# A Mamba-2 layer with a mixture of experts: where rows are finished, the last store goes out, and routing work stands

## What is computed

```python
xn = layernorm(x)                              # input of both branches
zxbcdt = xn @ in_proj_w.T                      # z 1024, x 1024, B 128, C 128, dt 16 (heads of 64)
xBC = silu(conv_b + causal_conv(xBC, 4 taps)); dt = softplus(dt + dt_bias)
# scan by chunks: Y_diag = ((C Bt) * L) (x dt);  Y_off = C state * exp(cumsum);  state = state * decay + Bt (x dt)
y = rmsnorm((Y_diag + Y_off + x * D) * silu(z)) * norm_w
attn = y @ out_proj_w.T
experts = sum over the top 2 of 8 experts of  weight * down(silu(gate(xn)) * up(xn))
out = x + attn + experts
```

## Time and profile before

| | us |
|---|---|
| runs, median of 3 | 699.69 (699.25 to 702.23) |
| profiled execution, its own time | 697.2 |
| its span | 695.2 |
| TensorE busy | 637.0 (92%) |
| VectorE busy | 507.8 (73%) |
| ScalarE busy | 373.6 (54%) |
| GpSimd busy | 294.0 (42%) |
| chain that ended last: TensorE, VectorE, issue, DMA | 61%, 17%, 7%, 7% |

### The profile page before, as it was taken

The page is one execution under the profiler, slowest core; times in us unless marked ns, Lnnn a source line. Parts: engine busy times, 40 slices in busy tenths (PEclk is TensorE's granted clock), DMA queues, the critical chain, the costliest instruction groups (busy, mean ns, idle before and its releaser), DMA issues.

```text
span 695.2 us, 12667 instructions
## 1 busy us (share of the span) xinstructions
PE 637.0 (92%) x4215; PEld 522.4 (75%) x4216; DVE 507.8 (73%) x1098; ACT 373.6 (54%) x787; POOL 294.0 (42%) x209
## 2 busy tenths in 40 slices
PE   4998899999999999989999989898988899999991
PEld 3896687868879678776877967665677788899981
DVE  6998868877977887787797698999786644444430
ACT  4778936564654754557376373638245444444431
POOL 2011344526435454453544424341136665656641
PEclk9999999999999999999999999998999999999996
DMA  8672014305113131530412304083594766767663
GB/s 269 231 288 92 1 39 145 122 11 173 60 64 122 62 123 32 151 123 1 152 51 103 96 28 130 1 272 115 172 305 80 132 123 117 125 120 123 125 100 45
DMA packets 31890, 80.38 MB, mean 116 GB/s; under 512 B 4768, under 2 KB 10016, under 8 KB 29664
## 3 DMA queue, kind: packets, MB, share of 16 engines
q1 hardware_dynamic: 22784, 58.23, 25.4%
q0 software_dynamic: 9056, 21.50, 17.1%
HBM read 59.93 MB, written 19.79 MB: 115 GB/s over the span
## 4 chain that ended last, share of the span: by engine, by line
PE 61%; DVE 17%; issue 7%; DMA 7%; ACT 5%; POOL 2%; SPq 0%; DVEq 0%; ACTq 0%; POOLq 0%
PE pi L1471 17%; PE po L1510 11%; PE pg L1685 9%; PE pd L1698 7%; DVE xs L959 5%; PE py L1566 3%; PE py L1573 3%; PE px L1668 2%; DMA out<-yo,idx 2%; DVE y L1244 2%; PE pxb L1557 2%; PE pxb L1588 2%; ACT m L675 1%; DMA m<-cs_d 1%; DMA out<-o 1%
## 5 line engine op out<-in xcount | busy, mean ns | idle before, releaser
L1471 PE MATMUL pi<-xh,whl 128*128 128x256 f32 x1152 | 165.1, 286 | 1.8 <-DVE zs L965 1.3
L1471 PEld LDWEIGHTS pi<-xh,whl 128*128 128x128 f32 x1152 | 146.3, 188 | 4.6 <-issue 2.4
L959 DVE SCALAR_TENSOR_TENSOR xs<-raw,conv_w,xs 128x256 f32<-128x256 f32 x240 | 112.1, 532 | 11.0 <-ACT xs L650 10.9
L1510 PE MATMUL po<-wo,y 128*128 128x512 f32 x256 | 114.8, 602 | 0.5 <-DVE y L1256 0.5
L1471 PE MATMUL pi<-xl,whl 128*128 128x256 f32 x576 | 91.7, 281 | 0.0
L1510 PEld LDWEIGHTS po<-wo,y 128*128 128x128 f32 x256 | 48.1, 193 | 55.4 <-issue 55.2
L551 POOL DMA_INDIRECT out<-yo,idx x39 | 62.0, 1590 | 61.2 <-ACT yo L817 32.4
L675 ACT ACTIVATE m<-m,cs_tok 128x128 f32<-128x128 f32 x256 | 79.7, 389 | 0.5
L1471 PEld LDWEIGHTS pi<-xl,whl 128*128 128x128 f32 x576 | 78.4, 188 | 0.0
L1685 PE MATMUL pg<-ew,xgh 128*128 x312 | 64.6, 349 | 0.0
L524 POOL TENSOR_TENSOR carry<-carry,cd 128x1024 f32<-128x1024 f32 x14 | 27.8, 1987 | 79.6 <-PE py L1566 79.6
(11 more groups left out here) (220 smaller groups left out, 1161.9 us busy)
## 6 DMA issues: line engine op xcount, KB each, us to landing
m<-cs_d SPq DMA_DIRECT2D x16, 1024.0 KB, 6.5
e<-cs_d SPq DMA_DIRECT2D x30, 256.0 KB, 4.6
ew<-in_w_gu SPq DMA_DIRECT2D x8, 768.0 KB, 9.5
w_as_read<-in_w_in SPq DMA_DIRECT2D x9, 512.0 KB, 8.3
res<-in_x SPq DMA_DIRECT2D x16, 256.0 KB, 2.8
out<-o SPq DMA_DIRECT2D x16, 256.0 KB, 2.0
xin<-in_x SPq DMA_DIRECT2D x6, 512.0 KB, 3.6
xn_d<-xin SPq DMA_DIRECT2D x6, 512.0 KB, 2.8
```

The lines of the kernel that those rows point to most:

```text
L959: dve.scalar_tensor_tensor(out=xs[par][:, b, :], in0=raw[:, b, k:k + GT], scalar=conv_w[:, b, k:k + 1], in1=xs[par][:, b, :], op0=ALU.mult ...
L1471: mm = pe.matmul(bank[:, hf, :], whl[:, weight(g, n), lo, k, hf * P:(hf + 1) * P], xx[:, k, :], start=k3 == 0, stop=k3 == 11)
L1510: mm = pe.matmul(po[:, :], y[:, b, :], wo[:, b, :], start=b == 0, stop=b == XB - 1)
```

## The change

- `finish(t - 1)` of the even tiles 2 to 12 stands behind `carried()` instead of ahead of `own(1)`. SyncE's `store(t - 1)` and `load_res(t)` of these tiles move into the next tile, behind its decay loads.
- ScalarE casts the weights of expert 0 in tile 15 behind the copy of B, not at the end of tile 14.
- `probabilities()` stands at the end of tile 13. `experts_of_tiles()` goes to tile 15, in two parts, around the last-but-one `finish`.
- Gathers 2 and 3 write to two buffers of their own, over the second x buffer, and wait for the scan's last read of it (yd = 32). Gathers 4 and 5 go ahead of the loop and wait for the transposes of tiles 0 and 1.
- The last rows are stored by GpSimd, behind gather 5, not by SyncE behind the last experts.

```diff
@@ sync, in the loop over t
                 if t > 1 and c == 1:
                     load_decays2(t)
+                    if t < T - 2:
+                        store(t - 2)
+                        load_res(t - 1)
...
-                if t:
+                if t and (c == 1 or t == T - 2):
                     store(t - 1)
                     load_res(t)
...
             load_expert(sp, 7)
-            store(T - 1)
-            sp.wait_ge(o_out, 16 * T)
+            sp.wait_ge(o_out, 16 * (T - 1))
@@ gpsimd
             def gather(j):
-                if j >= 2:
+                to, arrived = (xg_more, xg_more_in) if j in (2, 3) else (xg, xg_in)
+                if j in (2, 3):
+                    pool.wait_ge(yd, 2 * T)
+                elif j in (4, 5):
+                    pool.wait_ge(gtr, j - 3 + CR)
+                elif j > 5:
                     pool.wait_ge(gtr, j - 1 + CR)
-                pool.indirect_dma_start(xg[j % 2][:, :], None, xn_d,
+                pool.indirect_dma_start(to[j % 2][:, :], None, xn_d,
...
                 if j == 0:
-                    pool.wait_ge(o_out, 16 * T)
+                    pool.wait_ge(o_out, 16 * (T - 1))
+                    pool.wait_ge(last_out, 16)
...
-            for j in range(4):
+            for j in range(6):
                 gather(j)
-            factor(T - 1)
+                if j == 3:
+                    factor(T - 1)
+            pool.wait_ge(o_done, T)
+            pool.dma_start(out_t[T - 1], o[:, :]).then_inc(last_out, 16)
             for j in range(1, J + 2):
-                if j + 3 < J:
+                if 2 < j < J - 3:
                     gather(j + 3)
@@ scalar
                 if t == T - 1:
-                    gate_up_high(act, 1)
-                    down_high(act, 1)
+                    for e in range(2):
+                        gate_up_high(act, e)
+                        down_high(act, e)
...
-                    gate_up_high(act, 0)
-                    down_high(act, 0)
@@ vector: experts_of_tiles(part): 0 the comparison, its sum, eidx; 1 the steps of packed and landed, interleaved
                 if t == T - 1:
+                    experts_of_tiles(0)
                     variance(t - 1)
                     decayed(0)
                     finish(t - 1)
+                    experts_of_tiles(1)
                     table()
...
-                if t == T - 3:
-                    probabilities()
...
-                if 0 < t < T - 1:
+                if 0 < t < T - 1 and (c == 1 or t == T - 2):
                     finish(t - 1)
...
                 if 0 < t < T - 2:
                     carried()
+                    if c == 0:
+                        finish(t - 1)
                 if t == T - 3:
-                    experts_of_tiles()
+                    probabilities()
@@ tensor, turn(j, par, r)
-                pe.wait_ge(xg_in[par], r * 16 + 16)
+                rows = xg[par]
+                if static(j, 2, 3):
+                    pe.wait_ge(xg_more_in[par], 16)
+                    rows = xg_more[par]
+                elif static(j, 0, 1):
+                    pe.wait_ge(xg_in[par], 16)
+                else:
+                    pe.wait_ge(xg_in[par], r * 16)
```

More of the change, by code:

```diff
@@ L236, in block @@
         es = Area(nc, zs_at, sb.at)
+        xg_more = [Area(nc, second + i * D * 4, zs_at)(f"xg{2 + i}", [P, D]) for i in range(2)]
         hh = [es(f"hh{i}", [FH, 2, P], F32R) for i in range(2)]
@@ L296, in block @@
         op, ss, var_done, rstd_done = sem("op"), sem("ss"), sem("var_done"), sem("rstd_done")
-        o_done, o_out = sem("o_done"), sem("o_out")
+        o_done, o_out, last_out = sem("o_done"), sem("o_out"), sem("last_out")
         route_sem, e1, b1, picks_done, pos_done, pos_read = (sem("route"), sem("e1"), sem("b1"), sem("picks_done"),
@@ L305, in block @@
         gu_hi_done, d_hi_done, gu_lo_done, d_lo_done = sem("gu_hi"), sem("d_hi"), sem("gu_lo"), sem("d_lo")
-        xg_in = [sem(f"xg_in{i}") for i in range(2)]
+        xg_in, xg_more_in = [sem(f"xg_in{i}") for i in range(2)], [sem(f"xg_in{i}") for i in range(2, 4)]
         gtr, x_hi, x_lo, gu = sem("gtr"), sem("x_hi"), sem("x_lo"), sem("gu")
@@ L1150, in table, with experts_of_tiles @@
                 dve.tensor_tensor(prob[:, :], prob[:, :], given(5), ALU.add).then_inc(prob_done, 1)
-            def experts_of_tiles():
+            def experts_of_tiles(part):
                 by_step = ef[:, :].rearrange("o (i two) -> o two i", two=2)
                 low, high = slice(0, (J - 3) // 2), slice(1, (J - 1) // 2)
-                dve.wait_ge(tab_in_s, 16)
                 route.after()
[L1157 to L1164, removed]
+                if part == 0:
+                    route.step(dve.tensor_tensor(ecmp[:, :, :], tabc[0:1, TAB["tile"]].unsqueeze(2).broadcast_to([1, J, E]),
+                                                 end[0:1, :].unsqueeze(1).broadcast_to([1, J, E]), ALU.is_ge))
+                    route.after()
+                    route.step(dve.tensor_reduce(ef[:, 0:J], ecmp[:, :, :], AX.X, ALU.add))
+                    route.after()
+                    route.step(dve.tensor_scalar(ef[:, 0:J], ef[:, 0:J], float(E - 1), None, ALU.min))
+                    route.after()
+                    dve.tensor_copy(eidx[:, :], ef[:, 0:J]).then_inc(eidx_done, 1)
+                    return
+                route.step(dve.tensor_tensor(ecmp[:, 1:J, 0], ef[:, 1:J], ef[:, 0:J - 1], ALU.is_gt))
                 route.step(dve.scalar_tensor_tensor(out=pf[:, :], in0=by_step[:, 1, high], scalar=float(E),
@@ L1167, in experts_of_tiles @@
                 route.after()
+                route.step(dve.scalar_tensor_tensor(out=ecmp[:, 1:J, 1], in0=ecmp[:, 1:J, 0], scalar=16.0,
+                                                    in1=tabc[0:1, TAB["lag"]][:, 1:J], op0=ALU.mult, op1=ALU.add))
                 route.step(dve.scalar_tensor_tensor(out=pf[:, :], in0=pf[:, :], scalar=float(E),
@@ L1170, in experts_of_tiles @@
                 route.after()
+                dve.tensor_copy(landed[:, 1:J], ecmp[:, 1:J, 1]).then_inc(eidx_done, 1)
                 route.step(dve.scalar_tensor_tensor(out=pf[:, :], in0=pf[:, :], scalar=float(E),
@@ L1174, in experts_of_tiles @@
                 dve.tensor_copy(packed[:, :], pf[:, :]).then_inc(eidx_done, 1)
-                route.step(dve.tensor_tensor(ecmp[:, 1:J, 0], ef[:, 1:J], ef[:, 0:J - 1], ALU.is_gt))
-                route.after()
-                dve.wait_ge(ctap, 3 * CB * G)
-                route.step(dve.scalar_tensor_tensor(out=ecmp[:, 1:J, 1], in0=ecmp[:, 1:J, 0], scalar=16.0,
-                                                    in1=tabc[0:1, TAB["lag"]][:, 1:J], op0=ALU.mult, op1=ALU.add))
-                route.after()
-                dve.tensor_copy(landed[:, 1:J], ecmp[:, 1:J, 1]).then_inc(eidx_done, 1)
             statistics(0)
@@ L1667, in turn @@
                 for k in range(KD):
-                    tr = pe.transpose(px[par][:, k, :], xg[par][:, k * P:(k + 1) * P], ident[:, :])
+                    tr = pe.transpose(px[par][:, k, :], rows[:, k * P:(k + 1) * P], ident[:, :])
                 tr.then_inc(gtr, 1)
```

2 lines of the change are left out of this document (1 added, 1 removed).

## The result

The changed kernel took 690.84 us in the median of 4 runs (688.24 to 691.87), the kernel before 699.47 beside it: a ratio of 0.9886, interval 0.9846 to 0.9927. By the ratio that is 8.0 us or 1.1% faster, by the two medians 8.6, beyond what a measurement here can tell from no change. The forecast was 687.9, range 684 to 694. The profiled execution took 691.86 us, 5.3 less than the one before (span 689.9 against 695.2), where 11.8 less was forecast; the gain of the medians lies between. A single pair of executions is a rough measure here: the same kernel's profiled execution took 688.4 us in each of two later measurements, 8.8 less than the one before.

The account below looks back on a forecast made before the run. Bound by TensorE with VectorE's carry in even tiles, VectorE in tiles 13 to 15, GpSimd's accumulations at the experts' start. 4.0 + 2.8 + 5.0 = 11.8 us off a 699.69 median: 687.9 us, range 684.0 to 694.0.

Parts of the forecast that it names:

- Even tiles, 4.0 us: Scan tiles 2 to 12: finish moved behind carried() readies the carry 0.66 us earlier in six tiles, 4.0 us won.
- Rival 3: Even tiles: moved finish delays the next tile's x·dt and TensorE waits for it; 7.8 us left, 691.9; chance 0.08.
- Tiles 13 to 15, 2.8 us: End of the scan: moved routing work and earlier copy of B bring the gated half of y 2.8 us earlier.
- the worst case: Tile 13: probabilities() waits for both GpSimd passes over y and ends at 456.3, so 2.7 us are won.
- Experts' start, 5.0 us: Expert tiles 0 to 10: earlier gathers and last store let accumulation 0 go out 3.2 us earlier; 5.0 us won.
- the 8.7 us over the later pace: Experts' start: ten steps take 50.27 us against 41.6 at the later pace; about 3.5 us was to remain.
- The rule that was set aside: Experts' start: VectorE's two-port operations block GpSimd's DMA descriptors; store up to 1.75 us later, about 3.3 instead of 5.0.
- Rival 1: Experts' start: the last store's landing does not move, that part brings 0.7 to 1 us; 7.6 won, 692.1; chance 0.19.
- Rival 4: Tile 15: longer waits drop TensorE's clock to half; from 23.6 us so, the gain is eaten; slower, chance 0.04.

Follow-up runs that it names:

- e1_store_back: The changed kernel with the last rows stored by SyncE behind experts 6 and 7 again: 690.01 us, ratio 0.9889 to the kernel before.
- e10_gathers_back: e1_store_back with gathers 2 and 3 also put back into the two old buffers: 689.11 us, ratio 0.9884 to the kernel before.
- the shorter fillers: The changed kernel plus 7, 6 and 9 unused TensorE products in waits of tiles 12 and 15: 686.01 us, ratio 0.9814 to the kernel before.

## Why the prediction was right, and where it was not

**Even tiles, 4.0 us: right.** Waits of 1.00 us became 0.3 to 0.4, and the move measured 3.3 to 3.5 us by itself. Tiles 1 to 11, five moved pieces, brought 4.3 to 5.0 us, where the term had 3.3. Part of the surplus is the one that the text left open, "earlier decays can only win where one is late": VectorE's waits for the decay rows fell from 3.5 us in 3 waits to 1.8 in 3. The sixth, in tile 12, lost 1.2: TensorE's clock fell behind a wait of 1.83 us that had been there before. Where it stayed up, in e1_store_back, e10_gathers_back and with the shorter fillers, tile 12 to 13 took 28.3 us, the 0.7 less that the term had. Rival 3 came true in tile 13 alone, where TensorE waits 1.05 us for x·dt.

**Tiles 13 to 15, 2.8 us: right in its parts, not at its end.** Tile 13 to 14 gave 2.5 against 2.7, by the worst case that was taken. Tile 15 gave 1.3, not 0.5: VectorE idled there for 1.53, 1.56 and 0.26 us before and does not now, and the routing work takes about 2.3 of these 3.35 us. That the copy of B made this possible is not shown: with the casts ahead of it again the stretch is just as short. (The prediction's first paragraph has VectorE working without a pause from 445 to 498 us; two of these idle times, in the earlier trace rows, say otherwise, and its paragraph on tile 15 uses them rightly.) What was left out is the price behind it: where the text did name longer waits ("TensorE will wait longer here than before"), the last output product now takes 1.2 to 1.5 us more at the lower clock. Net 2.4 in the profile.

**Experts' start, 5.0 us: this is the step that failed,** by its size. It measured 1.7 us in the profile after and 2.3 to 2.8 in the others. The term was built on the landing of the last store: "Accumulation 0 then goes out 3.2 us earlier ... the next two follow it, and ScalarE's 6.3 us of waits nearly vanish". Accumulation 0 went out 2.6 us earlier by the gate/up product but 1.2 by the gated half: the store took 2.2 us less to land, and the finish ahead of it ended 0.7 us later by that half, not earlier, behind the slower output product. The next two did follow, and tile 10 with them. What failed is the rest of the sum, from 3.2 us of lead to 5.0: of the 8.7 us over the later pace only 3.5 were to remain, and 7.0 did, 5.8 to 6.3 in the repetitions. The first accumulations wait for one another at 5.6 us a piece, slower than TensorE's step of 4.16 us, so ScalarE keeps 3.2 us of its waits; the trace of before had these links already (accumulations at 522.72, 528.41 and 533.91 us). And VectorE's splits hold GpSimd's own instructions. Neither the store's engine, nor the gathers' buffers, nor their order moved the time by more than the traces can tell. The store landed earlier where the routing work stood in tile 15, a link that the prediction did not see; whether through the weights' loads stays open.

**The rule that was set aside.** The prediction said of the Trainium skill (SBUF — State Buffer, "A bandwidth-pool intuition that's wrong (but worth ruling out)") that "no row here shows a GpSimd DMA held so". That was an oversight. In the kernel before, one gather takes 2.35 us where the first five take 0.95 to 1.08, and VectorE's split starts 0.27 us before it:

```profile
530.31 2.35 POOL L539 DMA_INDIRECT xg<-xn_d,idx  x1 [0.30 <-issue]
```

Another, at 507.12 us, began 0.3 us ahead of a split and took its usual 0.95. The traces agree with the direction of the rule, in that GpSimd's DMA instructions stretch while VectorE splits; they stretch beside a VectorE operation that adds or subtracts two operands in SBUF. By the rule the term would have been 3.3 us, nearer to what came, but by luck: it had the store held, and the store's own instruction took 0.59 us beside a split in every profile where GpSimd issues it.

**The sum** was 11.8 against 5.3 in the profiled executions: 3.4 of the shortfall arose at the experts' start, 2.5 in tile 1, 1.9 in tile 12 and 1.4 before the first expert; 2.9 came back where tiles 1 to 11 and 15 gave more than their terms. Against the medians it was 2.9 us off: the profiled execution of before was 2.3 us under its median, the one of after 1.0 over. Sign and range held, in part by luck: the loss in tile 1 has nothing to do with the change, and the surplus of tiles 1 to 11 was not in the sum. Rival 1 came true in part: by the gated half the store landed 1.2 us earlier, where the forecast had 2.5 and the rival 0.4; and its number, 692.1, lies nearer to the result than the forecast does. Rival 4 was right in kind and small in size; its reading that the one drop before was short rested on two of its 6.8 us.

## What to carry to other kernels

A wait of 1 us on the busiest engine that comes back in every second iteration is worth its full length when a step that nobody waits for stands ahead of the releaser; it was the one term here that held both ways. Before a chain of serial transfers is credited with more than the gain of its first link, compare the length of its links with the step of the engine that it feeds. And where TensorE's waits get longer, ask for the granted clock behind each, in more than one execution: the same wait of 1.8 us had a slow spell behind it in some and none in others. Products without use that fit into such waits kept the clock up; their 3 us in the median are not clear of the spread.

## What was not expected of the hardware

Spells of some 3.4 us, some of twice that, at the granted clock's lower level, 1.2 GHz, came at places that differ from execution to execution: at 476 to 483 us in the profile before, at 72, 414, 468, 492 and 536 us in the profile after, but not at 72 us in its two repetitions, whose tile 1 comes 2.7 to 2.9 us sooner. Four of the five began 0.7 to 1.4 us behind the end of a wait of 1.83 to 2.41 us; the one at 468 us came after 12 us in which TensorE was busy throughout, and no row here explains it. So each costs 1.4 to 2.5 us where the engine is the bound, and they make up part of the spread of 3 to 9 us between runs of one kernel: of 22 runs of the kernel before, the fastest, 694.67 us, had a mean clock of 0.985 and the slowest, 703.78 us, one of 0.971. The Trainium skill (TensorE: Matmul & The Clock Gate, Part 1) ties the clock to TensorE's own activity; the traces agree in that fillers kept it up at the three places where they stood, in one profiled execution each of two kernels.

GpSimd's DMA instructions, 1.0 us for a gather and 1.6 for an accumulation when alone, took 1.9 to 3.2 and 4.18 us where one of VectorE's splits was running as they began, and went on 0.9 to 1.5 us beyond the end of the splits. An instruction that seems only to issue a transfer can be held for longer than most of the arithmetic around it.
